# One FFN head weighted by ScalarE in two passes, its sums partly made by VectorE, and the expert Gelu in one burst

## The chip, the cores and the metric

The kernel runs on one core of a Trainium2 chip. The time is that of one execution on the device, in microseconds (us); of the kernel before there are three runs, with a median of 1721.02 us (1718.32 to 1722.32). The engines of the core work in parallel, each through its own list of instructions, and meet at semaphores: TensorE (PE), VectorE (DVE), ScalarE (ACT), GpSimd (POOL) and SyncE (SP, which issues the transfers).

## What is computed

A transformer block over 16 sequences of 512 tokens with 128 channels, in fp32: windowed attention, then an FFN that picks experts by product keys. Only the FFN is touched by the change:

```python
xn = (x - mu) * rsqrt(var + eps) * gamma + beta          # over all rows
q = (xn @ w_q.T)...                                      # 2 halves, 8 heads
sim = einsum('pbnhd,hkpd->pbnhk', q, keys)               # 32 similarities per half and head
s, i = top_k(sim, 8)
all_scores = sx[..., :, None] + sy[..., None, :]         # pair sums of the two halves
scores, pk = top_k(all_scores, 8)                        # 8 of the 1024 experts per head
o = einsum('bnd,bnhkd->bnhk', inputs, key_in[idx])
o = gelu(o) * softmax(scores)
return einsum('bnhk,bnhkd->bnd', o, key_out[idx])
```

The kernel gathers nothing. For each token and head it makes all 1024 pair sums, gives each the weight exp(sum - max - ln Z) where the sum is at least the eighth largest and zero elsewhere, adds the weights of the 8 heads, multiplies them with Gelu of all 1024 expert products, and multiplies the result with key_out.

## The kernel before

The attention runs first (to about 700 us) and isn't touched. The FFN, function `ffn`, works on 64 tiles of 128 tokens, in 16 groups (`GROUPS`) of four tiles (`GT`); k is the tile's place in its group and j its number. Each engine runs the same loops, over groups, k and the heads h = 0 to 7, and what an engine does besides its main work is written by hand into slots: "at head h of tile k, first do this".

- POOL (L772 in `pair_sums`) makes the 1024 pair sums of each head from the tile's similarities SIM into one of 16 buffers SUM. It may write a buffer when the mask of the head 16 before is done (`sum_buffer_free`, L776).
- ScalarE (L873) makes exp(sum + bias) into one of two PSUM buffers E, with the bias NB of that head. It waits for the sum, and for the mask two heads before, which frees E. In its slots: the copy of the similarities (`sim_copy`, L800), the copy of the output (`finish`, L820), two copies of expert products per tile (`o_copy`, L811), twice per group a Gelu over four expert blocks with a table load before and after it (`gelus`, L806, L807), the small exp (L837) and the logarithm (L841) of the next tile's softmax, and once per group the normalised rows BNT (L815).
- VectorE (L965, called the mask here) compares the sums with the eighth largest (TOP) and multiplies by E, into one of eight buffers W. Its other work is `choose`, cut into parts, for the tile ahead: parts 0 to 3 are the sixteen sweeps of max-8 over 32 similarities (L909), part 4 the candidates (L916 to L921), part 5 the eight largest and their distance from the maximum, D8 (L926, L929), part 6 the sum Z (L932), part 7 the bias NB (L936). `EVEN_PARTS` and `ODD_PARTS` say at which head which part is done: an entry (1, 0) is part 0 for the next tile. `experts` (L948), at head 1, multiplies the weights of the tile before, which TensorE has turned and added in WT, with the Gelu values GE, into CT. M8X and TOP lie in PSUM (SMALL).
- TensorE turns each W into WT, eight transposes a head (L1033), and in its slots makes the similarities (L975), one expert block of 512 tokens at a time (`o_block`, L978) and the output product (L997, L1000). Similarities, expert blocks and output all pass through one PSUM bank, MB. WT has one buffer: the first transposes of a tile wait until CT of the tile before has been made.
- SP loads the rows and the turned rows of the next group and stores the outputs of the last (L754, L759, L763).

The expert products of the first group are made before the loops, in the E buffers, and read by Gelu straight from PSUM (L828, L988).

Of the kernel before, what the change touches and what calls it, by code (L numbers as in the profile page):

```python
# [29 lines left out]
ACT = mybir.ActivationFunctionType  # L30
# [634 lines left out]
WRING = 8  # L665

EVEN_PARTS = ((), (), (), (), ((1, 0), (1, 1), (1, 2), (1, 3), (1, 4), (1, 5), (2, 0), (2, 1)), (), ((1, 6),), ((1, 7),))
ODD_PARTS = ((), (), ((1, 2),), ((1, 3),), ((1, 4), (1, 5)), (), ((1, 6),), ((1, 7),))

SIM0 = 2  # L670
SLOT_A, SLOT_OUT, SLOT_SIM, SLOT_B = 0, 2, 4, 6
COPY_B, COPY_A, COPY_OUT, COPY_SIM = 1, 3, 5, 7


def ffn(nc, ctx, x1, x2T, KM, key_in, key_out, gb, ident, bnst, first, out):
# [6 lines left out]
    def sem(name):  # L682
# [23 lines left out]
    NB = [sb(f"NB{b}", [P, FH]) for b in range(2)]  # L706
    SUM = [sb(f"SUM{b}", [P, NE]) for b in range(RING)]
# [6 lines left out]
    SMALL = ps("SMALL", [P, 4, FH, TOPK])  # L714
# [5 lines left out]
             "experts_weighted out_product out_copied expert_product expert_copied gelu_ready "  # L720
             "out_stored ranked candidates top_ready top_less_max top_exp exp_sum log_sum bias_ready").split()
# [46 lines left out]

    def pair_sums(eng, j, h, q):
# [26 lines left out]
    def _(act):  # L796
# [5 lines left out]
        def gelus(g, b, half):  # L802

            act.wait_ge(S["expert_copied"], g * BLK + (half + 1) * 4)
            o = GE[b][:, 4 * half:4 * half + 4, :].rearrange("p e n -> p (e n)")
            nc.scalar.activation(o, o, ACT.Gelu).then_inc(S["gelu_ready"], 1)  # L806
            nc.scalar.preload_act_table_set("natural_log_exp_and_others")  # L807

        def o_copy(g, b, e):
            act.wait_ge(S["expert_product"], g * BLK + e + 1)  # L810
            nc.scalar.copy(GE[b][:, e, :], MB[:, :]).then_inc(S["expert_copied"], 1)  # L811
# [17 lines left out]
        act.wait_ge(S["expert_copied"], BLK)  # L829
        act.sem_inc(S["gelu_ready"], 2)  # L830
# [8 lines left out]
        def small_ln(j):  # L839
            act.wait_ge(S["exp_sum"], j + 1)  # L840
            nc.scalar.activation(LZ[:, :], Z[:, :], ACT.Ln).then_inc(S["log_sum"], 1)  # L841

# [3 lines left out]
        def group(g, b, more):  # L846
            for k in range(GT):
# [4 lines left out]
                for h in range(FH):  # L852
# [6 lines left out]
                    if h == COPY_B and k and more:  # L859
                        o_copy(g + 1, 1 - b, 2 * k - 1)  # L860
# [237 lines left out]
```

## Time and profile before

| | us |
|---|---|
| median of three runs | 1721.02 |
| profiled execution, its time | 1717.66 |
| its span, first to last instruction | 1715.9 |
| busy in the span: VectorE | 1502.3 |
| TensorE matmul | 1490.5 |
| POOL | 1330.6 |
| ScalarE | 1264.6 |
| costliest groups: pair sums on POOL (L772), 512 of them | 958.5 |
| masks on VectorE (L965), 512 | 641.9 |
| exps on ScalarE (L873), 512 | 566.6 |

The profile is of one execution. Busy time is the union of an engine's instructions, so instructions that overlap are counted once. A timeline row gives the start of an instruction (or of a run of like ones, xN), the time to the end of the last, and in brackets the time that the engine stood idle before it and what ended that. Releasers are inferred from semaphore events. The step from one instruction's start to the next one's is often shorter than the duration, because engines start the next while the last drains; where an engine is full, the steps add up to its time and the durations don't. The granted clock is TensorE's, in parts of 2.4 GHz.

### The profile page before, as it was taken

Reading aid. Unit: us, or ns where it says so; the run is one execution under the profiler, and the core shown is the slowest. Engines: PE = TensorE matmul, PEld = TensorE weight load, DVE = VectorE, ACT = ScalarE, POOL = GpSimd, SP = SyncE. Lnnn points to the kernel's source line nnn. Section 1 sums busy time; section 2 is a strip of 40 time slices with the busy share of each in tenths; the row PEclk is TensorE's granted clock in tenths of the full one; section 3 lists DMA queues with packets and bytes.
Section 4 is the critical chain, followed back from the end, with each engine's and each line's share of the span. In section 5 each row is a group of like instructions: output and inputs, shape, how many; then the busy total and the mean of one; then the engine's idle time right before and its main releaser. Section 6 shows DMA issues by size and latency. Waiting matters only on the chain.

```text
span 1715.9 us, 33034 instructions
## 1 busy us (share of the span) xinstructions
PE 1490.5 (87%) x10688; PEld 1029.4 (60%) x10688; DVE 1502.3 (88%) x4488; ACT 1264.6 (74%) x1741; POOL 1330.6 (78%) x1579
## 2 busy tenths in 40 slices
PE   3799999999999998678888888888888888888877
PEld 2355555555555554367667666676666766667766
DVE  3889999999999985389999999999999999999998
ACT  1166666666666666378888888888888888888885
POOL 1055555556655556499999999999999999999993
PEclk9799999999999999789999999999999999999999
DMA  5344445444555440100000000000000000000000
GB/s 139 88 99 105 109 111 118 111 110 103 119 113 111 103 103 22 62 1 19 1 20 20 1 19 19 7 13 19 19 1 20 20 1 19 19 8 13 14 7 7
DMA packets 73627, 86.37 MB, mean 50 GB/s; under 512 B 9872, under 2 KB 63760, under 8 KB 68752
## 3 DMA queue, kind: packets, MB, share of 16 engines
q1 hardware_dynamic: 73456, 84.27, 20.7%
q8 instruction: 85, 1.39, 0.4%
q14 instruction: 86, 0.70, 0.2%
HBM read 58.30 MB, written 25.95 MB: 49 GB/s over the span
## 4 chain that ended last, share of the span: by engine, by line
POOL 47%; issue 5%; ACT 3%; DVE 2%; PE 1%; ACTq 0%; DVEq 0%; SPq 0%
POOL SUM L772 47%; ACT E L873 2%; DVE W L965 2%; ACT L807 1%; ACT GE L806 0%; PE WT L1033 0%; PE MB L1000 0%; PE E L988 0%; DVE CT L948 0%; DVE M8Y L909 0%; DVE SMALL L926 0%; ACT L806 0%; ACT SIM L800 0%; PE MB L975 0%; DVE SMALL L909 0%
## 5 line engine op out<-in xcount | busy, mean ns | idle before, releaser
L772 POOL TENSOR_TENSOR SUM<-SIM 128x1024 f32<-128x1024 f32 x512 | 958.5, 1928 | 11.5 <-DVE W L965 7.9
L965 DVE SCALAR_TENSOR_TENSOR W<-SUM,SMALL,E 128x1024 f32<-128x1024 f32 x512 | 641.9, 1279 | 46.4 <-ACT E L873 44.7
L873 ACT ACTIVATE E<-SUM,NB 128x1024 f32<-128x1024 f32 x512 | 566.6, 1118 | 102.1 <-DVE W L965 86.9
L1033 PEld LDWEIGHTS WT<-idf,W 128*128 128x128 f32 x4096 | 497.3, 151 | 231.3 <-DVE W L965 120.6
L1033 PE MATMUL WT<-idf,W 128*128 128x128 f32 x4096 | 570.8, 292 | 69.3 <-DVE CT L948 38.0
L261 POOL TENSOR_SCALAR_AFFINE_SELECT PT<-PT 128x128 f32<-128x128 f32 (+1 forms) x1024 | 336.9, 355 | 257.8 <-ACT PT L355 224.2
L414 DVE CUSTOM_DVE_ANT_0 SY<-SY,bandf 128x384 f32<-128x384 f32 x512 | 273.3, 574 | 0.0
L355 ACT ACTIVATE PT<-TX 128x512 f32<-128x512 f32 x256 | 153.0, 598 | 113.6 <-PE TX L542 113.4
L429 DVE TENSOR_REDUCE mx<-SX 128x2 f32<-128x512 f32 x256 | 174.5, 682 | 59.8 <-PE SX L524 59.7
L357 ACT ACTIVATE PT<-TY 128x768 f32<-128x768 f32 x256 | 207.4, 810 | 3.7
L570 PE MATMUL PV<-PT,V 128*32 128x384 f32 (+1 forms) x2048 | 165.5, 441 | 2.6 <-POOL PT L261 2.4
L516 PE MATMUL SY<-K,Q 72*128 72x384 bf16 x512 | 144.0, 339 | 8.4 <-DVE mx L414 4.3
L542 PE MATMUL TY<-Q,K 75*128 75x384 bf16 x512 | 125.9, 328 | 11.5 <-ACT PT L357 10.4
L975 PE MATMUL MB<-KM,BNT 128*128 128x512 f32 x128 | 72.1, 645 | 71.2 <-ACT OUT L820 69.4
L1000 PE MATMUL MB<-KO,CT 128*128 128x128 f32 x1024 | 124.9, 275 | 1.1 <-DVE CT L948 1.1
L516 PE MATMUL SX<-K,Q 72*128 72x256 bf16 x512 | 102.0, 281 | 24.4 <-DMA Q<-q_parts 18.9
L1000 PEld LDWEIGHTS MB<-KO,CT 128*128 128x128 f32 x1024 | 119.5, 192 | 1.3 <-DVE CT L948 1.3
L542 PE MATMUL TX<-Q,K 75*128 75x256 bf16 x512 | 99.6, 276 | 3.9 <-ACT PT L355 2.7
L948 DVE TENSOR_TENSOR CT<-WT,GE 128x1024 f32<-128x1024 f32 x64 | 78.4, 1225 | 20.2 <-PE WT L1033 20.2
L542 PEld LDWEIGHTS TX<-Q,K 75*128 75x128 bf16 x512 | 37.6, 98 | 97.2 <-issue 82.2
L570 PEld LDWEIGHTS PV<-PT,V 128*32 128x32 f32 x2048 | 53.6, 109 | 68.1 <-issue 47.9
L516 PEld LDWEIGHTS SX<-K,Q 72*128 72x128 bf16 x512 | 48.7, 100 | 67.3 <-issue 18.6
(110 smaller groups left out, 1638.9 us busy)
## 6 DMA issues: line engine op xcount, KB each, us to landing
K<-k_parts SPq DMA_DIRECT2D x96, 192.0 KB
Q<-q_parts SPq DMA_DIRECT2D x288, 64.0 KB
q_parts<-qp SPq DMA_DIRECT2D x16, 384.0 KB, 2.4
k_parts<-kp SPq DMA_DIRECT2D x16, 384.0 KB, 2.4
xin<-in_x SPq DMA_DIRECT2D x16, 256.0 KB, 3.1
xres<-in_x SPq DMA_DIRECT2D x16, 256.0 KB, 9.5
x<-X SPq DMA_DIRECT2D x16, 256.0 KB, 2.2
x2T<-X2T SPq DMA_DIRECT2D x16, 256.0 KB, 2.1
```

Of the source, the lines that this page charges most:

```text
L261: return nc.gpsimd.affine_select(out=out, in_=out, compare_op=ALU.is_ge, fill=0.0, base=0, pattern=([[0, 2]] if pairs else []) + [[s, P]], ...
L357: nc.scalar.activation(pt[:, 512:1280].rearrange("p (j n) -> p j n", j=2), TY[:, :, 0:384], ACT.Exp).then_inc(S["inner_exp"], 1)
L414: return nc.vector.tensor_tensor_reduce(out=scores, in0=scores, in1=bandf[:, k0 * P:k1 * P], scale=1.0, scalar=-3e38, op0=ALU.add, op1=ALU ...
L429: nc.vector.tensor_reduce(mx[:, h, 0:4:3], SX[:, :, :], AX.X, ALU.max).then_inc(S["outer_maxima"], 1)
L516: return pe.matmul(out, Q[b][0:KQ, h, i * P:(i + 1) * P], K[b][0:KQ, h, k0 * P:k1 * P], start=clear, stop=done, skip_group_check=True)
L542: return pe.matmul(out[:, 0:(q1 - q0) * P], K[b][0:R, h, j * P:(j + 1) * P], Q[b][0:R, h, q0 * P:q1 * P], start=True, stop=True, skip_grou ...
L570: o = pe.matmul(PV[32 * e:32 * e + 32, q0 * P:q1 * P], V[b][:, slot:slot + SLOT_V], PT[:, h % 8, at:at + (q1 - q0) * P], start=(j == 0 and ...
L772: return eng.tensor_tensor(SUM[(q * FH + h) % RING][:, :].rearrange("p (i j) -> p i j", i=NK), sx, sy, ALU.add)
L873: nc.scalar.activation(E[h % 2][:, :], SUM[(k * FH + h) % RING][:, :], ACT.Exp, bias=NB[q][:, h:h + 1]).then_inc(S["exp_ready"], 1)
L965: nc.vector.scalar_tensor_tensor(out=W[h % WRING][:, :], in0=SUM[(k * FH + h) % RING][:, :], scalar=TOP[q][:, h, TOPK - 1:TOPK], in1=E[h % ...
L1000: o = pe.matmul(po, CT[k % 2][:, e, :], key_out[:, e, :], start=False, stop=(e == BLK - 1))
L1033: o = pe.matmul(WT[:, e, :], W[h % WRING][:, e * P:(e + 1) * P], ident[:, :], is_transpose=True, start=(h == 0 and e % 4 == 0), stop=(h == ...
```

## The change

One head of the eight, LH = 3, is no longer masked by VectorE. ScalarE reads its sums in place with Prelu, bias minus the eighth largest (NT) and alpha 1e30, so that sums below the eighth largest become hugely negative and the others their distance from it; then exp with the bias NL, which is D8 of the eighth largest less ln Z, writes W directly. VectorE makes the two biases: NT in part 5, NL in part 7. There are so seven masks a tile, and the exps of a tile alternate over the two E buffers by their own count.

In the tiles with k = 3 and k = 0 (tile 0 excepted, 31 in all) the pair sums of that head are made by VectorE and not by POOL, in two new parts: part 8 copies the 32 similarities of one half to PSUM (XL), part 9 makes the 1024 sums from XL and SIM.

The expert products of the next group are no longer made two a tile through MB and copied. At k = 2, after head 0's exp, TensorE makes all eight one after another in the halves of the two E buffers (`experts_in`), and ScalarE, between two table loads, reads each with Gelu into GE (`experts_gelu`). To go with it, the ranking parts are placed anew: three tables instead of two, with a long list at head 1 of tile k = 2. SP's list isn't changed.

```diff
+LH = 3
+MASKED = FH - 1
+SUMS_AHEAD = (2, 3)
+BURST = 2
+NORMAL_PARTS = ((), (), ((1, 0), (1, 1)), ((1, 2), (1, 3)), ((1, 4), (1, 5)), (), ((1, 6),), ((1, 7),))
+BURST_PARTS = ((), ((1, 0), (1, 1), (1, 2), (1, 3), (1, 4), (1, 5), (1, 8), (2, 0), (2, 1), (2, 2), (2, 3), (2, 4), (1, 9)), (), (), (), (), ((1, 6),), ((1, 7),))
+LATER_PARTS = ((), (), ((1, 8),), ((1, 9),), ((1, 5),), (), ((1, 6),), ((1, 7),))
+PARTS = (NORMAL_PARTS, NORMAL_PARTS, BURST_PARTS, LATER_PARTS)
...
+    XL = SMALL[:, 4, 0:NK // TOPK, :].rearrange("p a b -> p (a b)")
...
     def sum_buffer_free(eng, j, h):
-        wait_pos(eng, S["weights_masked"], j * FH + h - RING + 1)
+        if h == LH:
+            wait_pos(eng, S["l_weights"], j - 1)
+        else:
+            wait_pos(eng, S["weights_masked"], masked(j - 2, h))
...
                 for h in range(FH):
+                    if h == LH and sum_by_vector(j):
+                        continue
                     sum_buffer_free(pool, j, h)
...
+        def experts_gelu(j, g, b):
+
+            wait_pos(act, S["experts_weighted"], (g - 1) * GT)
+            nc.scalar.preload_act_table_set("gelu_and_others")
+            for e in range(BLK):
+                act.wait_ge(S["expert_product"], g * BLK + e + 1)
+                nc.scalar.activation(GE[b][:, e, :], expert_bank(j, e), ACT.Gelu).then_inc(S["expert_copied"], 1)
             nc.scalar.preload_act_table_set("natural_log_exp_and_others")
+            act.wait_ge(S["expert_copied"], (g + 1) * BLK)
...
+        def l_shift(j, k, q):
...
+            s = SUM[(k * FH + LH) % RING][:, :]
+            nc.scalar.activation(s, s, ACT.Prelu, bias=NT[q][:, :], alpha=1e30).then_inc(S["l_shifted"], 1)
+
+        def l_exp(j, k, q):
+
+            act.wait_ge(S["l_shifted"], j + 1)
+            wait_pos(act, S["weights_turned"], (j - 1) * FH + LH + 1)
+            nc.scalar.activation(W[LH][:, :], SUM[(k * FH + LH) % RING][:, :], ACT.Exp, bias=NL[q][:, :]).then_inc(S["l_weights"], 1)
...
+                    if h == 1 and k == BURST and more:
+                        experts_gelu(j, g + 1, 1 - b)
...
+                    if h == LH - 1:
+                        l_shift(j, k, q)
+                    if h == LH:
+                        l_exp(j, k, q)
...
+                nc.vector.tensor_scalar(NT[q][:, :], TOP[q][:, LH, TOPK - 1:TOPK], -1.0, None, ALU.mult)
...
             if part == 7:
                 dve.wait_ge(S["log_sum"], j + 1)
-
+                nc.vector.tensor_tensor(NL[q][:, :], D8[:, LH, TOPK - 1:TOPK], LZ[:, LH:LH + 1], ALU.subtract)
...
+            if part == 8 and sum_by_vector(j):
+
+                nc.vector.tensor_copy(XL, SIM[r][:, 0, LH, :]).then_inc(S["l_x_moved"], 1)
+            if part == 9 and sum_by_vector(j):
+
+                dve.wait_ge(S["l_x_moved"], sums_by_vector(j))
+                wait_pos(dve, S["l_weights"], j - 1)
+                nc.vector.tensor_tensor(SUM[(r * FH + LH) % RING][:, :].rearrange("p (i j) -> p i j", i=NK),
+                                        XL.unsqueeze(2).broadcast_to([P, NK, NK]),
+                                        SIM[r][:, 1, LH, :].unsqueeze(1).broadcast_to([P, NK, NK]), ALU.add).then_inc(S["l_sums"], 1)
...
+        def experts_in(j, g, b):
+
+            for e in range(BLK):
+                if e == 0:
+                    pe.wait_ge(S["x2T_loaded"], (g + 1) * 16)
+                    pe.wait_ge(S["weights_masked"], j * MASKED)
+                if e == 2:
+                    pe.wait_ge(S["weights_masked"], j * MASKED + 1)
+                if e >= 4:
+                    pe.wait_ge(S["expert_copied"], g * BLK + e - 3)
+                pe.matmul(expert_bank(j, e), key_in[:, e * P:(e + 1) * P], X2T[b][:, :], start=True, stop=True).then_inc(S["expert_product"], 1)
```

## Rows read from the trace of the kernel before

**Rows 1.** The page: busy time of each engine, and the chain that ended last.

```profile
PE 1490.5 (87%) x10688; PEld 1029.4 (60%) x10688; DVE 1502.3 (88%) x4488; ACT 1264.6 (74%) x1741; POOL 1330.6 (78%) x1579
...
POOL 47%; issue 5%; ACT 3%; DVE 2%; PE 1%; ACTq 0%; DVEq 0%; SPq 0%
```

**Rows 2.** Timeline of POOL; columns: start us, length us, engine, line, operation, count, idle.

```profile
720.35 636.25 POOL L772 TENSOR_TENSOR SUM<-SIM 128x1024 f32<-128x1024 f32 x340 [3.54 <-ACT SIM L800]
...
1357.30 29.98 POOL L772 TENSOR_TENSOR SUM<-SIM 128x1024 f32<-128x1024 f32 x16 [0.70 <-DVE W L965]
```

**Rows 3.** Timeline of DVE, two tiles of the steady state (same columns).

```profile
1344.14 2.48 DVE L965 SCALAR_TENSOR_TENSOR W<-SUM,SMALL,E 128x1024 f32<-128x1024 f32 x2 [0.49 <-ACT E L873]
...
1346.61 1.23 DVE L948 TENSOR_TENSOR CT<-WT,GE 128x1024 f32<-128x1024 f32 x1
...
1347.75 3.81 DVE L965 SCALAR_TENSOR_TENSOR W<-SUM,SMALL,E 128x1024 f32<-128x1024 f32 x3
...
1351.48 0.84 DVE L909 MAX8 SMALL<-SIM 128x8 f32<-128x32 f32 x8
...
1354.69 0.84 DVE L909 MAX8 SMALL<-SIM 128x8 f32<-128x32 f32 x8
...
1355.94 2.49 DVE L965 SCALAR_TENSOR_TENSOR W<-SUM,SMALL,E 128x1024 f32<-128x1024 f32 x2 [0.41 <-ACT E L873]
...
1358.47 1.28 DVE L965 SCALAR_TENSOR_TENSOR W<-SUM,SMALL,E 128x1024 f32<-128x1024 f32 x1
...
1360.33 2.48 DVE L965 SCALAR_TENSOR_TENSOR W<-SUM,SMALL,E 128x1024 f32<-128x1024 f32 x2 [0.50 <-ACT E L873]
```

**Rows 4.** Timeline of ACT over the same two tiles.

```profile
1350.26 1.28 ACT L806 ACT_TABLE_LOAD   x1
...
1351.56 1.91 ACT L806 ACTIVATE GE<-GE 128x2048 f32<-128x2048 f32 x1
...
1354.78 1.12 ACT L873 ACTIVATE E<-SUM,NB 128x1024 f32<-128x1024 f32 x1
...
1359.18 2.16 ACT L873 ACTIVATE E<-SUM,NB 128x1024 f32<-128x1024 f32 x2
...
1361.65 0.59 ACT L811 COPY GE<-MB 128x512 f32<-128x512 f32 x1 [0.32 <-PE MB L978]
```

**Rows 5.** Timeline of ACT at the start of the FFN.

```profile
721.41 0.60 ACT L828 ACTIVATE GE<-E 128x512 f32<-128x512 f32 x1 [0.26 <-PE E L988]
...
724.84 0.60 ACT L828 ACTIVATE GE<-E 128x512 f32<-128x512 f32 x1 [0.26 <-PE E L988]
```

**Rows 6.** Timeline of PE over the two tiles of Rows 3.

```profile
1350.24 1.95 PE L1000 MATMUL MB<-KO,CT 128*128 128x128 f32 x16
...
1356.24 1.39 PE L975 MATMUL MB<-KM,BNT 128*128 128x512 f32 x2 [2.30 <-ACT OUT L820]
...
1357.43 3.33 PE L1033 MATMUL WT<-idf,W 128*128 128x128 f32 x16
...
1361.45 1.91 PE L1033 MATMUL WT<-idf,W 128*128 128x128 f32 x16
```

**Rows 7.** Windows, PE: length us, busy us (instructions), granted clock, DMA share, GB/s.

```profile
1357.50:1358.00 0.50, 0.50 (x4) 0.50 1.01 281
```

**Rows 8.** Instructions of two lines of the attention: duration ns min/median/max.

```profile
L404 DVE SCALAR_TENSOR_TENSOR rm<-MB,mp x32: 274/274/278, 63.7 to 664.7; 32x128 f32<-32x128 f32 x32
...
L410 DVE TENSOR_TENSOR mp<-rm,mp x32: 274/354/510, 67.1 to 667.0; 32x128 bf16<-32x128 f32 x32
```

**Rows 9.** Timeline of DVE and POOL in the attention.

```profile
365.39 0.69 DVE L477 TENSOR_TENSOR qp<-rq,qp 128x512 bf16<-128x512 f32 x1
...
366.07 0.55 POOL L261 TENSOR_SCALAR_AFFINE_SELECT PT<-PT 128x128 f32<-128x128 f32 x2 [0.78 <-ACT PT L355]
```

**Rows 10.** Timeline of DVE, last group of four tiles.

```profile
1651.18 2.48 DVE L965 SCALAR_TENSOR_TENSOR W<-SUM,SMALL,E 128x1024 f32<-128x1024 f32 x2 [0.49 <-ACT E L873]
...
1709.62 1.23 DVE L948 TENSOR_TENSOR CT<-WT,GE 128x1024 f32<-128x1024 f32 x1 [1.19 <-PE WT L1033]
```

More of the change, by code:

```diff
@@ L706, in ffn @@
     NB = [sb(f"NB{b}", [P, FH]) for b in range(2)]
+    NT = [sb(f"NT{b}", [P, 1]) for b in range(2)]
+    NL = [sb(f"NL{b}", [P, 1]) for b in range(2)]
     SUM = [sb(f"SUM{b}", [P, NE]) for b in range(RING)]
@@ L767, in _, with sum_by_vector, sums_by_vector, sums_by_pool @@
         store(GROUPS - 1, 1)
+    def sum_by_vector(j):
+        return j > 0 and (j - 1) % GT in SUMS_AHEAD
+    def sums_by_vector(j):
+        return sum(sum_by_vector(i) for i in range(j + 1))
+    def sums_by_pool(j, h):
+        return j * FH + h + 1 - sums_by_vector(j if h >= LH else j - 1)
+    def masked(j, h):
+        return j * MASKED + (h if h >= LH else h + 1)
+    def expert_bank(j, e):
+        return E[(j * MASKED + 1 + e // 2) % 2][:, e % 2 * GN:(e % 2 + 1) * GN]
     def pair_sums(eng, j, h, q):
@@ L857, in group @@
                         bnt(g + 1, 1 - b)
-                    if h == COPY_B and k and more:
-                        o_copy(g + 1, 1 - b, 2 * k - 1)
-                    if h == COPY_B and not k and real:
-                        o_copy(g, b, BLK - 1)
-                    if h == COPY_A and more:
-                        if k == 0:
-                            wait_pos(act, S["experts_weighted"], g * GT)
-                        o_copy(g + 1, 1 - b, 2 * k)
+                    if h == 1 and k == BURST and more:
+                        experts_gelu(j, g + 1, 1 - b)
                     if h == COPY_OUT and (real or k):
@@ L878, in group @@
                         small_ln(j + 1)
-                    if (k, h) == (2, 3) and more:
-                        gelus(g + 1, 1 - b, 0)
-                    if (k, h) == (0, 3) and real:
-                        gelus(g, b, 1)
         steps(act, group)
@@ L945, in experts @@
             dve.wait_ge(S["weights_turned"], (j + 1) * FH)
-            dve.wait_ge(S["gelu_ready"], (g + 1) * 2)
+            dve.wait_ge(S["expert_copied"], (g + 1) * BLK)
             wait_pos(dve, S["out_product"], j - 1)
@@ L956, in group @@
                 for h in range(FH):
-                    for ahead, part in (ODD_PARTS if k % 2 else EVEN_PARTS)[h]:
+                    if h == 1 and real:
+                        experts(*prev)
+                    for ahead, part in PARTS[k][h]:
                         if more or k < GT - ahead:
                             choose(part, j + ahead, (k + ahead) % 4, (k + ahead) % 2)
-                    if h == 1 and real:
-                        experts(*prev)
-                    dve.wait_ge(S["exp_ready"], j * FH + h + 1)
+                    if h == LH:
+                        continue
+                    n = masked(j, h)
+                    dve.wait_ge(S["exp_ready"], n)
                     wait_pos(dve, S["weights_turned"], j * FH + h - WRING + 1)
                     nc.vector.scalar_tensor_tensor(out=W[h % WRING][:, :], in0=SUM[(k * FH + h) % RING][:, :], scalar=TOP[q][:, h, TOPK - 1:TOPK],
-                                                   in1=E[h % 2][:, :], op0=ALU.is_ge, op1=ALU.mult).then_inc(S["weights_masked"], 1)
+                                                   in1=E[(n - 1) % 2][:, :], op0=ALU.is_ge, op1=ALU.mult).then_inc(S["weights_masked"], 1)
         steps(dve, group)
```

53 lines of the change are left out of this document (21 added, 32 removed).

## The prediction, made before the changed kernel was run

> **What bounds the kernel now.** I read the page first. Its chain of work that ended last gives POOL 47% of the span [rows 1], so at first sight the pair sums of POOL are the bound and every sum taken off it is time won. The timeline of POOL says otherwise. The first 340 sums of the FFN run without a gap in 636.25 us, 1.87 us each, which is 15.0 us for the eight of a tile; after that POOL runs 16 sums in 29.98 us and then stands 0.70 us until the mask of L965 frees a buffer of the ring of 16, and this pair of tiles, 30.68 us, repeats to the end [rows 2]. So POOL was ahead from the start, filled its ring, and is then held back by its consumer: the FFN runs at 15.34 us a tile, set by VectorE and ScalarE together, not at POOL's 15.0.
>
> The timeline of VectorE shows how these two hold each other. The exps go into two PSUM buffers, so an exp may start only when the mask two before it has ended. One mask takes 1.28 us, and the next instruction starts 1.20 us after it; an exp takes 1.12 us and the next starts 1.04 us after it [rows 3, 4]. With masks alone this loop keeps up (1.2 to 1.27 us a head). Whatever ScalarE does between two exps, while VectorE has nothing but masks, is lost: 1.86 us instead of 1.2 pass from mask 6 (1358.47) to mask 7 (1360.33; mask h is that of head h, 0 to 7), because a logarithm and a copy of 512 columns stand between the exps [rows 3]. Where VectorE has other work, ScalarE's extra is hidden: two table loads and a Gelu of 2048 columns, from 1350.26 to 1354.78, cost VectorE only 0.41 us [rows 3, 4].
>
> **The change, part by part.** I lay out one group of four tiles, counting each tile from the start of one mask 7 to the start of the next; four tiles take 61.4 us now (twice 30.68). Steps come from rows 3 unless another group is named. After mask 7: 1.20 to the next tile's mask 0, 1.27 to the expert product CT (L948), 1.14 to mask 1. The ranking for the next tile (parts 0 to 5) takes 3.21 (1351.48 to 1354.69), about 0.8 of it for each eight max-8 (0.84) and 1.6 for candidates and top. Mask 4 to mask 6: 2.53 (1355.94 to 1358.47).
>
> *Head 3 moved to ScalarE.* Per tile it takes one mask, 1.20, off VectorE and adds there two instructions of one column, which I take at 0.1 each, the step of one max-8 (what the second may wait for is costed below). ScalarE gets two passes of 1.04 in place of one. In an ordinary tile these are hidden: VectorE then has CT, 1.14, and 3.2 us of ranking between its masks.
>
> *Ordinary tiles (k = 0 and 1).* 1.20 + 1.27 + 1.14 + 1.20 (mask 1) + 0.80 + 1.20 (mask 2) + 0.85 + 0.65 + 1.00 (ranking, with the new small instruction) + 2.53 (mask 4 to mask 6) + 1.86 = 13.7 us each. ScalarE is ready in time: exp 1 begins at 1.35, when mask 7 has ended, the shift pass at 2.4, exp 2 runs from 3.45 to 4.6, and mask 2 comes at 5.6.
>
> *Sums made by VectorE (for k = 3 and k = 0, 31 in all).* Each takes 1.87 off POOL, which is worth nothing by itself, since POOL is not the bound. It costs VectorE a tensor_tensor of 1024 columns with one input in PSUM, like CT (1.23, step 1.14), and a copy of 32 columns, about 0.12. Tile k = 3: 1.20 + 1.27 + 1.14 + 1.20 + 0.12 + 1.20 + 1.14 (sum) + 0.95 (part 5) + 2.53 + 1.86 = 12.6.
>
> *The Gelu burst (k = 2).* Eight copies of 0.59, two Gelus of 1.91 and four table loads per group go; eight Gelus of 0.60 and two loads come. That is 6 us less ScalarE work a group, but now it stands in one piece in which no exp can be made, because its products lie in the exps' own PSUM buffers. TensorE: the transposes of head 7 begin when mask 7 has ended, at 1.35, and take 0.95 (16 in 1.91 [rows 6]); then eight products. At the start of the FFN the same products come to ScalarE's Gelu one each 0.857 us (721.41 to 724.84 is four) [rows 5], not one each 0.5 as ScalarE could take them. The last Gelu so ends at 2.3 + 7 x 0.857 + 1.02 + 0.64 = 10.0, the load after it at 11.3 (1.28 to 1.31 for a load) [rows 4], exp 1 at 12.45 (1.02 is one product alone: 0.86 and the last pass's tail, and 0.64 the Gelu with its start). VectorE has meanwhile done mask 0, CT and the ranking moved here (3.3 + 2.0 + 0.2 + the sum of 1.14), and is idle from 10.2 to 12.45. After that ScalarE is behind and VectorE has masks alone: shift pass, exp 2, second pass, exp 4 follow at 1.05 each, so that mask 4 comes at 16.7; the copy of OUT waits for transposes (0.95) and output products (2.2) that TensorE starts only when mask 1 has ended at 13.8, so it comes at 17.0, mask 5 at 18.3, mask 6 at 19.6, and after logarithm and copy of SIM mask 7 at 21.4 [rows 4, 6]. So 21.4 us.
>
> Sum of a group: 13.7 + 13.7 + 12.6 + 21.4 = 61.4 us, against 61.4 now. What three tiles win, the burst tile loses. At the ends: group 0 wins 0.2 (its first tile has no CT), the last group has no burst: 13.7 + 13.2 (no copy of SIM) + 14.5 (the ranking for k = 3 and its sum, 4.6 us, ahead of mask 1, then masks paced by the exps) + 11.9 (no ranking) = 53.3, against 56.0 now (1651.18 to the last CT at 1709.62, less the 2.47 between mask 7 and CT [rows 10]), so 2.7. By these steps alone: 3 us less.
>
> *TensorE's clock.* After the burst TensorE stands idle from 10.25 to 13.8, 3.5 us. In the kernel before, after a standstill of 2.30 us, the granted clock is 0.50 (1.2 instead of 2.4 GHz) and 16 transposes take 3.33 us instead of 1.91 [rows 6, 7]. There this lies beside work that hides it. In the burst tile it lies on the path: the OUT copy, the fifth exp and all behind it wait. Price between 0 and 1.8 us; I take the row's difference, 1.4, in 15 groups: +21 us.
>
> *The new bias NL (part 7 of choose).* This one-column tensor_tensor reads D8 and LZ, both in SBUF. No VectorE instruction of the FFN does so now while POOL is at work: each has one input in PSUM. The attention shows what it means. L404 and L410 have one shape, 32x128; L404 (one input in PSUM) takes 274 to 278 ns, L410 (both in SBUF) 274 to 510, median 354; it is the longer where a POOL instruction of 0.4 us is under way [rows 8]. And where L477, both in SBUF, runs for 0.69 us from 365.39, POOL's next instruction begins at 366.07, at its end [rows 9]. So they exclude each other for a whole instruction. The Trainium skill, "SBUF — State Buffer", section "Who interferes with whom", says the same: a VectorE instruction with two SBUF inputs and a GpSimd one that reads SBUF share a read interface, and whichever starts first keeps it to its end. In the FFN a POOL instruction lasts 1.87 us and the next follows at once. NL waits between 0 and 1.87; mask 7 (now 1.86 after mask 6, of which 1.2 is mask 6 itself) and, through NB, the next tile's exp absorb 0.4 of it. Over an even spread the mean of what is left is 1.47 squared / 2 / 1.87 = 0.58 us a tile, 37 us in 64 tiles. Bounds: 0 (POOL idle at that point, or one column too short to matter) and 1.47 x 64 = 94.
>
> Forecast: 1717.7 (the profiled execution) - 3 + 21 + 37 = 1773. The median of the runs lies 3.4 above that execution, so 1776.
>
> One rule speaks against the burst more strongly still. A load here is followed by its activation within 0.03 us (1350.26 + 1.28, next 1351.56) [rows 4]. The Trainium skill, "ScalarE: Activation LUTs", section "What ACT_TABLE_LOAD costs", adds 1.38 us of drain to each; with that the two loads of a burst would cost 2.8 us more on the path, some 41 us in all. The row decides; I leave it out.
>
> **Rivals.**
> (a) Only the clock, no lock: an instruction of one column slips in between. 1717.7 + 18, as a median 1739. For it: nothing so short is in the trace beside a busy POOL. Chance 0.20.
> (b) Neither: TensorE's pause falls so that the clock stays up. 1718 as a median, within 0.2%. Chance 0.08.
> (c) Faster: ScalarE isn't late after the burst. If the masks after it came at VectorE's pace, the burst tile would cost its VectorE work, 7 x 1.20 + 1.14 + 6.6 + 0.5 = 16.6, plus the 2.3 of standstill, 18.9 instead of 21.4: 15 x 2.5 = 37 us less, about 1680 without the lock. Against it: the 1.05 of each exp and two extra passes are plain rows. Chance 0.13.
> (d) The lock at its worst: POOL's and VectorE's periods lock in a bad phase, a wait near 1.87 in most tiles: 1773 + 40 = 1813 and up. Chance 0.07.
> (e) Prelu isn't in the set that holds exp and logarithm: two loads a tile, 64 x 2.6 = 166 us more, about 1900. No row shows a Prelu. Chance 0.04.
> Forecast itself 0.48.
>
> **How the numbers follow.** A difference of 0.2% is about what a measurement of this kernel can tell from none. Slower: forecast 0.48, (a) 0.20, (d) 0.07, (e) 0.04, less a little that falls near zero, 0.76. Same: most of (b), 0.07. Faster: (c) and the rest of (b), 0.17. Range 1714 to 1812: from (b) to the edge of (d); it leaves out (c), (e) and part of (d), about 2 in 10.
>
> **What would show it.** Right: groups of 63 to 66 us in VectorE's timeline; in tile k = 2 masks 1, 2 and 4 at 12.5, 14.6 and 16.7 after the mask 7 before; transposes after the burst at a granted clock of 0.5; NL with durations spread from 0.16 to 2 us; POOL idle some 5 us or more a group. Wrong: NL at 0.16 everywhere (then a); products in the burst faster than 0.857; a table load at the Prelu's line; POOL without idle time, which would mean that its sums bound the kernel after all.

## The result and the profile of the kernel after

The changed kernel takes 1866.84 us (median of four runs, 1865.28 to 1866.94). The kernel before, run beside it on the same chip, takes 1719.67 (1713.83 to 1722.32). The ratio is 1.0859, with a 95% interval of 1.0829 to 1.0888: 147 us slower. The forecast was 1776 in a range of 1714 to 1812: right in direction and in the two causes it named, too low by 91 us.

The page of the kernel after: busy time, granted clock in 40 slices, the chain that ended last, and the groups that matter.

```profile
PE 1507.1 (81%) x10688; PEld 1072.1 (57%) x10688; DVE 1595.7 (86%) x4614; ACT 1235.8 (66%) x1745; POOL 1274.8 (68%) x1548
...
PEclk9799999999999997789889889889889889889888
...
PE 22%; DVE 21%; issue 15%; ACT 4%; DVEq 0%; ACTq 0%; SPq 0%
...
L802 POOL TENSOR_TENSOR SUM<-SIM 128x1024 f32<-128x1024 f32 x481 | 904.5, 1914 | 209.9 <-DVE W L1023 206.1
L1095 PE MATMUL WT<-idf,W 128*128 128x128 f32 x4096 | 566.7, 293 | 273.6 <-DVE W L1023 203.0
...
L979 DVE TENSOR_TENSOR NL<-D,LZ 128x1 f32<-128x1 f32 x64 | 135.9, 2123 | 0.3 <-ACT LZ L873 0.3
```

Beside [rows 1] three things stand out. VectorE is busy for 1595.7 us in place of 1502.3, although it lost 64 masks: 135.9 us of that are 64 instructions on one column each (L979, the new bias NL), which therefore last 2.12 us on average. The chain no longer runs through POOL at all. And POOL stands idle for 206 us in its sums' line, held back by the masks (L1023).

The timeline of VectorE shows what NL does. Columns as in the rows of before: start, length, engine, line, operation, count, idle before it.

```profile
1300.80 1.18 DVE L979 TENSOR_TENSOR NL<-D,LZ 128x1 f32<-128x1 f32 x1
...
1313.77 1.29 DVE L1023 SCALAR_TENSOR_TENSOR W<-SUM,SMALL,E 128x1024 f32<-128x1024 f32 x1
1314.97 5.70 DVE L979 TENSOR_TENSOR NL<-D,LZ 128x1 f32<-128x1 f32 x1
1320.59 0.15 DVE L980 SCALAR_TENSOR_TENSOR NB<-LZ,SMALL 128x8 f32<-128x8 f32 x1
1320.66 2.54 DVE L1023 SCALAR_TENSOR_TENSOR W<-SUM,SMALL,E 128x1024 f32<-128x1024 f32 x2
1323.99 1.23 DVE L1003 TENSOR_TENSOR CT<-WT,GE 128x1024 f32<-128x1024 f32 x1 [0.79 <-PE WT L1095]
...
1335.93 0.77 DVE L979 TENSOR_TENSOR NL<-D,LZ 128x1 f32<-128x1 f32 x1
```

POOL over the same stretch.

```profile
1286.95 33.70 POOL L802 TENSOR_TENSOR SUM<-SIM 128x1024 f32<-128x1024 f32 x18 [1.37 <-DVE W L1023]
1322.01 3.78 POOL L802 TENSOR_TENSOR SUM<-SIM 128x1024 f32<-128x1024 f32 x2 [1.36 <-DVE W L1023]
```

The NL that starts at 1314.97 ends at 1320.67, and POOL's run of 18 sums ends at 1320.65: VectorE has stood still while POOL ended one sum and made three more. The NL at 1300.80 ends at 1301.98, eight sums of 1.87 after 1286.95: it waited for the running sum alone. NL never ends anywhere but at the end of a sum, unless POOL stands idle (once, 0.15 us). Of the 64, 51 take between 0.77 and 1.78 us, eleven 5.69 to 5.72, and one, at 755.71 when POOL still fills its ring, 18.75. Everything behind it waits too: the exps stand idle for NB, 104.7 us in all.

The burst tile (k = 2): ScalarE, then TensorE, then VectorE.

```profile
1337.95 1.28 ACT L840 ACT_TABLE_LOAD   x1
1340.02 0.60 ACT L843 ACTIVATE GE<-E 128x512 f32<-128x512 f32 x1 [0.79 <-PE E L1045]
...
1346.03 0.60 ACT L843 ACTIVATE GE<-E 128x512 f32<-128x512 f32 x1 [0.26 <-PE E L1045]
1346.64 1.28 ACT L844 ACT_TABLE_LOAD   x1
1347.94 1.12 ACT L920 ACTIVATE E<-SUM,NB 128x1024 f32<-128x1024 f32 x1
```

```profile
1350.43 1.09 PE L1095 MATMUL WT<-idf,W 128*128 128x128 f32 x8 [3.57 <-DVE W L1023]
...
1351.62 3.54 PE L1067 MATMUL MB<-KO,CT 128*128 128x128 f32 x16
```

```profile
1349.09 1.28 DVE L1023 SCALAR_TENSOR_TENSOR W<-SUM,SMALL,E 128x1024 f32<-128x1024 f32 x1 [2.17 <-ACT E L920]
1351.16 1.29 DVE L1023 SCALAR_TENSOR_TENSOR W<-SUM,SMALL,E 128x1024 f32<-128x1024 f32 x1 [0.79 <-ACT E L920]
1353.24 1.28 DVE L1023 SCALAR_TENSOR_TENSOR W<-SUM,SMALL,E 128x1024 f32<-128x1024 f32 x1 [0.79 <-ACT E L920]
1356.52 1.28 DVE L1023 SCALAR_TENSOR_TENSOR W<-SUM,SMALL,E 128x1024 f32<-128x1024 f32 x1 [2.00 <-ACT E L920]
```

Here the layout of the prediction is found step by step: a Gelu each 0.859 us, paced by its product, as in [rows 5]; VectorE idle for 2.17 us, forecast 2.3; then masks 2.07 apart, forecast 2.1; TensorE idle for 3.57 us, forecast 3.5, and behind that pause a granted clock of 0.50 (a window from 1352.0 to 1354.5), at which the output product takes 3.54 us in place of 1.95. The eight transposes right behind the pause still ran at 0.98 (a window from 1350.0 to 1351.6); the low clock came after them. A load is followed by its exp after 1.30 us, as in [rows 4]; the 1.38 us of drain that the Trainium skill adds in "ScalarE: Activation LUTs", section "What ACT_TABLE_LOAD costs", are in no load of the burst either. The Prelu starts at 1348.99, 1.05 us after that exp, with no load at its line, so rival (e) is out, and the masks 2.07 apart rule out rival (c).

### The profile page after: what moved, and what is told of

Its sections match the earlier page's. It is cut to its first block, busy times and chain, and to the rows that moved or that the text cites. A ratio compares the mean times of both kernels' runs of the same rounds, so it can differ in the third digit from the quotient of the medians.

```text
span 1865.2 us, 32977 instructions
## 1 busy us (share of the span) xinstructions
PE 1507.1 (81%) x10688; PEld 1072.1 (57%) x10688; DVE 1595.7 (86%) x4614; ACT 1235.8 (66%) x1745; POOL 1274.8 (68%) x1548
## 4 chain that ended last, share of the span: by engine, by line
PE 22%; DVE 21%; issue 15%; ACT 4%; DVEq 0%; ACTq 0%; SPq 0%
DVE W L1023 12%; PE WT L1095 10%; PE E L1045 6%; PE MB L1067 5%; ACT E L920 3%; DVE NL L979 2%; DVE CT L1003 1%; DVE SMALL L969 1%; DVE SMALL L952 1%; DVE M8Y L952 1%; PE MB L1064 1%; DVE SUM L989 1%; DVE Z L976 1%; DVE NB L980 1%; PE E L1055 0%
## 5 line engine op out<-in xcount | busy, mean ns | idle before, releaser
L802 POOL TENSOR_TENSOR SUM<-SIM 128x1024 f32<-128x1024 f32 x481 | 904.5, 1914 | 209.9 <-DVE W L1023 206.1
L1023 DVE SCALAR_TENSOR_TENSOR W<-SUM,SMALL,E 128x1024 f32<-128x1024 f32 x448 | 569.5, 1279 | 114.8 <-ACT E L920 114.5
L920 ACT ACTIVATE E<-SUM,NB 128x1024 f32<-128x1024 f32 x448 | 498.7, 1114 | 134.7 <-DVE NB L980 104.7
L1067 PE MATMUL MB<-KO,CT 128*128 128x128 f32 x1024 | 149.9, 309 | 1.1 <-DVE CT L1003 1.1
L1067 PEld LDWEIGHTS MB<-KO,CT 128*128 128x128 f32 x1024 | 146.5, 228 | 1.3 <-DVE CT L1003 1.3
L979 DVE TENSOR_TENSOR NL<-D,LZ 128x1 f32<-128x1 f32 x64 | 135.9, 2123 | 0.3 <-ACT LZ L873 0.3
L854 ACT COPY OUT<-MB 128x128 f32<-128x128 f32 x64 | 17.0, 265 | 143.2 <-PE MB L1067 143.2
L843 ACT ACTIVATE GE<-E 128x512 f32<-128x512 f32 x120 | 71.7, 597 | 42.1 <-PE E L1045 42.1
```

The lines of the kernel that those rows point to most:

```text
L802: return eng.tensor_tensor(SUM[(q * FH + h) % RING][:, :].rearrange("p (i j) -> p i j", i=NK), sx, sy, ALU.add)
L920: nc.scalar.activation(E[(n - 1) % 2][:, :], SUM[(k * FH + h) % RING][:, :], ACT.Exp, bias=NB[q][:, h:h + 1]).then_inc(S["exp_ready"], 1)
L1023: nc.vector.scalar_tensor_tensor(out=W[h % WRING][:, :], in0=SUM[(k * FH + h) % RING][:, :], scalar=TOP[q][:, h, TOPK - 1:TOPK], in1=E[(n ...
L1067: o = pe.matmul(po, CT[k % 2][:, e, :], key_out[:, e, :], start=False, stop=(e == BLK - 1))
```

## The experiments

Three suspects: NL's wait for POOL, TensorE's clock, and the rest of the reordering. A tile's time below is the distance of its CT (L1003) from the CT before, read from VectorE's timeline; four are a group, given in the order k = 2, 3, 0, 1.

### e1: NL without a second SBUF input

The first one-column operand of NL is put into PSUM, by one more instruction of one column in part 5.

```diff
+    DP = SMALL[:, 4, NK // TOPK, 0:1]
...
+                nc.vector.tensor_tensor(DP, TOP[q][:, LH, TOPK - 1:TOPK], CD[:, LH, 0:1], ALU.subtract)
...
-                nc.vector.tensor_tensor(NL[q][:, :], D8[:, LH, TOPK - 1:TOPK], LZ[:, LH:LH + 1], ALU.subtract)
+                nc.vector.tensor_tensor(NL[q][:, :], DP, LZ[:, LH:LH + 1], ALU.subtract)
```

> The changed kernel with one thing different: the bias NL is made from the distance of the eighth largest in PSUM (one more one-column instruction in part 5) and ln Z in SBUF, so that it has one SBUF input. Theory 1 (the whole loss beyond the forecast is the wait of this instruction for POOL): its mean falls from 2.12 us to about 0.15 us, the waits of 5.7 and 18.8 us vanish, and the time falls by some 105 to 125 us of 1867, to 1740 to 1760, where my sum without the lock had 1739. Rival (the long durations only cover other waits, for exps or ring buffers, which then show up elsewhere): the time falls by less than 40 us.

Measured 1768.5 us, ratio to before 1.0296 (1.0277 to 1.0316). Every NL now takes 0.15 us; the row gives duration min/median/max:

```profile
L981 DVE TENSOR_TENSOR NL<-SMALL,LZ x64: 150/152/157, 729.4 to 1743.2; 128x1 f32<-128x1 f32 x64
```

That is 97 us less, by (1.0859 - 1.0296) x 1719, where 105 to 125 were expected. So the lock costs 97 us in this kernel, whatever it does to TensorE's clock included. The same from the durations: 135.9 less 64 x 0.15 is 126 us of waiting, of which 97 reach the end, so that 29 us, 0.45 a tile, are absorbed (the prediction had 0.4). But 1768 is 50 us above before, where a clock term of 21 and a gain of 3 had left room for 18. Its steady tiles take 22.97, 14.0, 14.0 and 13.9, 64.9 a group.

### e2: the lock alone, in the kernel before

The kernel before with that one instruction added in part 7; nothing reads its result.

```diff
+                nc.vector.tensor_tensor(NL[q][:, :], D8[:, 3, TOPK - 1:TOPK], LZ[:, 3:4], ALU.subtract)
```

> The kernel before with one instruction added, the same one-column tensor_tensor of two SBUF inputs in part 7 of each tile (its result is used by nothing). Theory 1, first half (it waits for the end of the POOL instruction under way, 1.87 us at most): mean duration about 1.0 us, 0.6 us a tile lost, 1720 to about 1757. Theory 1, second half (if it comes just before such an end it misses it, and then gets no turn until POOL itself pauses): some durations of many times 1.87 us, more so early, where POOL has the ring to fill; mean 2 us or more, time 1790 or more. Rival (the cost belongs to something else of the change): durations of 0.16 us and about 1723.

Measured 1773.49 us, ratio 1.0328 (1.0302 to 1.0354). The 64 add up to 115 us: nearly all are 1.42 to 1.44 and 1.70 to 1.73 by turns, and one is 18.52. The steady tiles go from 13.90 and 16.82 to 14.96 and 16.95, so they lose 1.06 and 0.13, 0.6 on average. The prediction's formula gives 0.58 for a wait of at most one sum, but from an even spread of waits with 0.4 absorbed, and neither is found here: that the two agree is luck. 0.6 a tile is 37 us; the one long wait accounts for the other 19.

```profile
759.66 18.52 DVE L936 TENSOR_TENSOR NL<-D,LZ 128x1 f32<-128x1 f32 x1
```

```profile
738.90 39.26 POOL L773 TENSOR_TENSOR SUM<-SIM 128x1024 f32<-128x1024 f32 x21
779.52 3.78 POOL L773 TENSOR_TENSOR SUM<-SIM 128x1024 f32<-128x1024 f32 x2 [1.36 <-DVE W L966]
```

759.66 + 18.52 is 778.18, the end of POOL's run is 778.16. The ring held sums that POOL could go on making without VectorE, and it made them all. This NL began 1.71 us before the next end of a sum, so a start just before an end is not what brings a long wait on.

### e3: are VectorE's sums worth anything?

e1 with all sums on POOL again (no head in which VectorE makes them).

```diff
-SUMS_AHEAD = (2, 3)
+SUMS_AHEAD = ()
```

> As e1, but no sums by VectorE: POOL makes all 512. Theory: with the lock gone, a group takes about 61 to 63 us, POOL needs 60.0 for its 32 sums, so POOL is nearly the bound; VectorE saves two sums and two copies, 2.5 us a group, of which about 1.2 (tile k = 3, where it is full) would have been on the path, and POOL's limit takes it back: within 10 us of e1. Rival (POOL's sums bound the kernel, as its chain of before suggests): 30 us or more slower than e1.

Measured 1769.6 us, ratio 1.0313 (1.0292 to 1.0334): the same as e1. (The profiled run is the fastest of the five, 1756.9; the others took 1767 to 1772.) POOL makes 512 sums instead of 481 and still stands idle for its consumer, so it never was the bound, as the prediction had read from [rows 2]. This run shows something else as well. It runs two of its early groups in 61.4 us each (21.39, 12.59, 13.71, 13.72) and all from 1186 us on in 64.9 (22.97, 13.99, 14.00, 13.90), with the same instructions in the same order. What differs is the clock: 1.00 over the first two, 0.89 over the later ones.

### e4: TensorE kept busy in the pause after the burst

e1 with four products of 512 columns on TensorE, added work without use, written to the free bank MB after the expert products and head 0's transposes in the burst tile.

```diff
+FILL = 4
...
+                    if h == 1 and k == BURST and more:
...
+                        for _ in range(FILL):
+                            pe.matmul(MB[:, :], ident[:, :], key_in[:, 0:GN], start=True, stop=True)
```

> As e1, with four products of 512 columns added on TensorE into the idle bank MB, in the burst tile between head 0's and head 1's transposes, 3.4 us of work in a pause of 3.6 us; their result is overwritten. Theory (the low clock after the pause costs 1.4 us a group): output product after the burst in 1.95 us, not 3.54; 15 to 25 us faster than e1. Rival (the late exps after the burst are set by ScalarE's own work, not by the output product): same as e1 within 4 us.

Measured 1724.34 us, ratio 1.0045 (1.003 to 1.006), mean granted clock 0.979 (e1 0.933). Its tiles are 21.39, 12.66, 13.71 and 13.72: the prediction's 21.4, 12.6, 13.7 and 13.7. So the layout had every tile right, and the low clock costs (1.0296 - 1.0045) x 1718 = 43 us in e1, not 21. Where, the timeline of TensorE shows, first e1, then e4.

```profile
1325.78 3.49 PE L1097 MATMUL WT<-idf,W 128*128 128x128 f32 x16 [1.41 <-DVE CT L1005]
...
1349.57 1.97 PE L1097 MATMUL WT<-idf,W 128*128 128x128 f32 x8 [3.57 <-DVE W L1025]
```

```profile
1336.54 2.19 PE L1103 MATMUL WT<-idf,W 128*128 128x128 f32 x16 [1.41 <-DVE CT L1006]
...
1349.25 2.19 PE L1103 MATMUL WT<-idf,W 128*128 128x128 f32 x16 [1.41 <-DVE CT L1006]
```

At the change of tiles TensorE stands for 0.7 us and then for 1.41, waiting for CT. In e1 the 16 transposes behind that ran at 0.50 of the clock (a window from 1326.0 to 1329.0) and took 3.49 us, in e4 2.19 at 1.00 (1336.6 to 1338.7). CT and the output copy sit behind those too. The fill in the burst tile removes the low clock not only there but at nearly all tile changes. In e1 its burst tile loses 22.97 - 21.39 = 1.6 us (the prediction had 1.4) and the three others 14.0 - 12.66, 14.0 - 13.71 and 13.9 - 13.72 = 1.8 us: the half that the prediction did not have.

In the kernel after itself, with the lock in place, the low clock lies in part elsewhere. A tile change like these runs at 1.00 there (a window from 1305.9 to 1308.0), and the 0.50 (1322.1 to 1331.0) stands behind the pause that a long wait of NL makes:

```profile
1305.81 2.19 PE L1095 MATMUL WT<-idf,W 128*128 128x128 f32 x16 [1.41 <-DVE CT L1003]
...
1321.99 1.97 PE L1095 MATMUL WT<-idf,W 128*128 128x128 f32 x8 [5.79 <-DVE W L1023]
1325.37 3.65 PE L1095 MATMUL WT<-idf,W 128*128 128x128 f32 x16 [1.41 <-DVE CT L1003]
```

So 97 and 43 are the two losses taken out in this order. No run of the changed kernel has the lock without the low clock, and in the other order the split could differ.

### e5: NL a little later

The kernel after with two instructions of one column, which touch no second SBUF input, ahead of NL.

```diff
+                for i in range(2):
+                    nc.vector.tensor_scalar(NX[:, 2 * q + i:2 * q + i + 1], TOP[q][:, LH, TOPK - 1:TOPK], -1.0, None, ALU.mult)
```

> The changed kernel, with two one-column instructions of VectorE (PSUM to SBUF, result unused) ahead of NL, which moves NL 0.14 us later. In the changed kernel the waits of 5.7 us all begin 0.07 us before a POOL instruction ends, and all others begin at least 0.6 us before one and end with it. Theory 1 (a request that comes just before the end of a POOL instruction misses it and then gets no turn until POOL pauses): moved past that end, these waits become 1.8 us, NL's sum falls from 136 us to 80 to 105, and the kernel gets 25 to 50 us faster in spite of the added work. Rival (the long waits belong to that tile, k = 1, or to a long stream of POOL, and not to the moment): they stay at 5.7 us and the time is that of the changed kernel or a few us more.

Measured 1870.95 us, ratio 1.0881 (1.0842 to 1.0921). The theory was that the long waits are a matter of 0.1 us, because in the kernel after the long-waiting NLs start 0.08 to 0.10 us ahead of the end of a sum. It fell. They now start 0.07 to 0.11 after the next sum has begun, and wait to the same point as before:

```profile
1323.91 5.56 DVE L982 TENSOR_TENSOR NL<-D,LZ 128x1 f32<-128x1 f32 x1
```

```profile
1295.76 33.70 POOL L803 TENSOR_TENSOR SUM<-SIM 128x1024 f32<-128x1024 f32 x18 [2.45 <-DVE W L1026]
```

(1323.91 + 5.56 = 1329.47, 1295.76 + 33.70 = 1329.46.) Again eleven of 5.55 to 5.58, and one of 18.61.

### e8: POOL with fewer sums ready

The kernel after; each of POOL's sums waits for the masks of two heads more than its buffer needs.

```diff
+LESS = 2
...
-        else:
-            wait_pos(eng, S["weights_masked"], masked(j - 2, h))
+        wait_pos(eng, S["weights_masked"], masked(j - 2, h) + LESS)
```

> The changed kernel; GpSimd alone is held back: before each sum it waits for the weights of two heads more than its data needs, so that fewer sums with their waits already met stand ready on its queue. In the changed kernel 12 of the 64 NL operations got their turn only after three or more of GpSimd's operations (5.7 us eleven times, 18.75 once), and in all of these GpSimd had at least three ready sums; where at most two were ready VectorE got its turn at the end of the running operation. Theory A, the length of the wait is the number of sums that stand ready: the waits of 5.7 us and the long one vanish, NL's sum falls from 136 us to some 60 to 90, and the time from 1867 to some 1810 to 1835 us. Theory B, the length comes from the place in the group (a group's second tile), not from what stands ready: the eleven waits of 5.7 us stay, NL's sum stays over 120 us and the time within 15 us of 1867. GpSimd's smaller lead can cost some us of its own, since each of its sums starts later by two heads; the sums' readers (the next layer's projections) show it if it does.

Measured 1872.38 us, ratio 1.0907 (1.0876 to 1.0939). (The sums' readers are ScalarE's exps; there is no next layer here.) Neither theory holds as put. The waits of 5.7 us are gone, as A said, but their sum isn't down: 131.7 us. In their place stand 15 waits of 3.50 to 3.84 us, ten of 1.96 to 1.99 and one of 15.01. What holds is the end of the long ones: all 16 over 3 us end within 0.03 us of the end of an unbroken run of POOL, behind which it stands idle for its next mask. That it takes three ready sums is wrong, since here one or two went ahead of VectorE; and in the kernel after the first two NLs waited for one end only (1.78 and 1.24 us) with about ten sums ready. The ten waits of 1.96 to 1.99 are a third kind: NL starts some 0.08 us before the end of a sum, is passed over there, and gets its turn at the next end, although POOL has more sums ready.

```profile
894.78 1.96 DVE L979 TENSOR_TENSOR NL<-D,LZ 128x1 f32<-128x1 f32 x1
```

```profile
877.99 35.55 POOL L803 TENSOR_TENSOR SUM<-SIM 128x1024 f32<-128x1024 f32 x19 [0.21 <-DVE W L1023]
```

The tenth sum of this run ends at 896.7, the NL at 896.74, and nine more sums follow without a gap. One more thing differs in this kernel: the sum of head 3 has two waits ahead of it, the others one. Wherever that sum came next at the end of the one under way, NL got its turn (30 times, these ten among them); the long waits end elsewhere, behind sums with one wait.

### e9: shorter instructions on POOL

The kernel after with each sum made by two instructions of 512 columns.

```diff
...
+        n = NK // 2
+        for a in (0, n):
+            sx = SIM[q][:, 0, h, a:a + n].unsqueeze(2).broadcast_to([P, n, NK])
...
+            last = eng.tensor_tensor(SUM[(q * FH + h) % RING][:, a * NK:(a + n) * NK].rearrange("p (i j) -> p i j", i=n), sx, sy, ALU.add)
```

> The changed kernel with each of GpSimd's pair sums made by two instructions of 512 columns each, of which only the second reports; same data, same waits, same places. It shows whether NL's wait is counted in GpSimd's instructions or in the work that stands ready. Theory A, a number of instructions passed over: every wait halves, the eleven of 5.70 us become some 2.9, the sum of the 64 falls from 136 us to some 70, and the time by some 45 to 55 us, to 1815. Theory B, VectorE, once passed over, gets its turn only when GpSimd has nothing ready: the waits of 5.7 us stay (three sums ready are six instructions), only the short ones (54 us in all, 0.77 to 1.8 each, the rest of one instruction) halve; the sum is about 108 us and the time about 1845. Against either: if one half takes over 0.95 us the sums cost GpSimd more than 1.87 us each, and over some 1.8 in place of 1.87 for two halves its slack of a group shrinks; at 1.05 a half GpSimd (30 sums a group, 63 us) is still under a group's 72 us.

Measured 1901.71 us, ratio 1.1077 (1.1022 to 1.1131): slower yet, against both. POOL makes a half each 1.01 us. The 64 NL add up to 156.3 us. The short waits did halve: 48 of them are 0.15 to 0.94. There are more long ones: fifteen of 4.77 to 8.60, and 24.26 at the start.

```profile
1338.66 8.58 DVE L982 TENSOR_TENSOR NL<-D,LZ 128x1 f32<-128x1 f32 x1
```

```profile
1311.01 36.21 POOL L804 TENSOR_TENSOR SUM<-SIM 128x512 f32<-128x512 f32 x36 [1.22 <-DVE W L1026]
1348.59 4.06 POOL L804 TENSOR_TENSOR SUM<-SIM 128x512 f32<-128x512 f32 x4 [1.37 <-DVE W L1026]
```

1338.66 + 8.58 = 1347.24, POOL's run ends at 1347.22, and nine of its instructions have ended in between. So the long wait is not a number of instructions: all 16 end with POOL's run, as in theory B (e8's ten short passings stay the exception). B's time (1845) is missed: more NLs are passed over (16 instead of 12), and two halves take 2.01 us in place of 1.87, so that POOL's run of ready work is longer. How much each of the two adds was not separated. Two NLs of this run had the same picture before them, 0.75 us to the next end and four halves ready, and waited 4.78 us (at 897.13) and 0.76.

### e6b, e6, e7: the rest of the loss, and a version that beats both

All three have e1's NL. e6b also makes the burst tile's output product right after head 0's transposes and no longer behind those of head 1, so that it is itself the work that fills TensorE's pause. e6 besides moves the two passes of head 3 ahead of the Gelus. e7 besides puts one product of 512 columns without use ahead of head 0's transposes in the other tiles.

```diff
                     if h == 1 and k == BURST and more:
+                        l_shift(j, k, q)
+                        l_exp(j, k, q)
                         experts_gelu(j, g + 1, 1 - b)
...
-                    if h == SLOT_OUT and real:
+                    if h == (1 if k == BURST and more else SLOT_OUT) and real:
...
+                        if real and not (k == BURST and more):
...
+                            for _ in range(FILL):
+                                pe.matmul(MB[:, :], ident[:, :], key_in[:, 0:GN], start=True, stop=True)
```

> As e1 (NL with one input in PSUM), and in the burst tile TensorE makes the output product one slot earlier, between head 0's and head 1's transposes, in its pause of 3.6 us. Theory: the pause shrinks to about 1.3 us, so the clock stays up behind it, and the OUT copy no longer waits; burst tile 21.1 us instead of 22.97. If the other tiles keep the full clock too, some 1720; if they fall to it as in e1 (14.0 instead of 12.6 and 13.7), up to 1745. Rival (the output product was late for another reason than its place): as e1.

Measured 1719.21 us, ratio 1.001 (0.9993 to 1.0026); burst tile 20.95, against 21.1 expected, and the tile behind it 12.65.

> As e6b_out_early, and in the burst tile both passes of head 3 on ScalarE stand ahead of the Gelu burst instead of behind it. Theory (the burst is paced by TensorE's products, 0.857 us each, so 2.1 us of ScalarE work ahead of it are hidden, and behind it ScalarE is what everything waits for): second exp at 12.45 as now, burst tile 19.3 us, 15 x 1.8 to 2.1 = 27 to 32 us faster than e6b_out_early, about 1690 to 1715 and so faster than the kernel before. Rival (the burst ends later by what is put ahead of it): same as e6b within 5 us.

Measured 1701.95 us, ratio 0.9897 (0.9877 to 0.9918); burst tile 19.45, since two passes that stood among the late exps after the burst are now done in front of it. That is 17 us less than e6b, where 27 to 32 were expected: the burst tile gains 1.5 us and not 1.8 to 2.1, and in four groups the tile k = 3 took 13.99 in place of 12.65.

> As e6_early, and in every other tile TensorE makes one product of 512 columns into the idle bank MB in the pause before head 0's transposes (0.86 us of a pause of 1.41 us; its result is overwritten). Theory (the pauses of 0.66 and 1.41 us around the change of tile are enough to lower the clock when they fall together as they did in e1): mean granted clock up to 0.98 and up to 20 us faster than e6_early, all tiles at 13.7, 12.7 and 19.3. If e6_early has the full clock already: equal to it.

Measured 1693.15 us (1690.26 to 1698.35), ratio 0.985 (0.9824 to 0.9877), clock 0.984; tiles 19.44, 12.65, 13.71 and 13.72, 59.5 a group against 61.4 in before. In e6 some tiles still took 13.99 in place of 12.65; in e7 none of the steady ones does. TensorE's pause of 1.41 us at the tile change is so filled but for 0.1 us on either side of the product:

```profile
1338.95 1.09 PE L1106 MATMUL WT<-idf,W 128*128 128x128 f32 x8 [0.76 <-DVE W L1029]
1340.15 1.13 PE L1102 MATMUL MB<-KI,idf 128*128 128x512 f32 x2
1341.37 2.29 PE L1106 MATMUL WT<-idf,W 128*128 128x128 f32 x16
```

All three ideas of the change are still in e7 (the head on ScalarE, the sums on VectorE, the burst), and with three losses taken out (the lock, the low clock, the late passes after the burst) it is 1.5% faster than the kernel before and 9.3% faster than the kernel after.

## Why the prediction was wrong in size

The 147 us, by the ratios and in the order in which they were taken out: 97 for the lock (e1), 43 for the clock (e4), 8 for the rest. The prediction had 37, 21 and -3.

*The bound.* Right. POOL isn't it: e3 gives its 31 sums back at no cost, and in the kernel after it stands idle for 206 us.

*The layout of the four tiles.* Right, to 0.1 us in each (e4), and with it the sentence that three tiles win what the burst tile loses. The one tile that it had wrong is k = 2 of the last group, which has no burst: 14.5 forecast, 18.93 measured in e1 and e4. There ScalarE stands for the output product, and this behind transposes that TensorE makes at a low clock after a pause of 4.7 us (e4):

```profile
1691.48 1.97 PE L1103 MATMUL WT<-idf,W 128*128 128x128 f32 x8 [4.73 <-DVE W L1026]
...
1693.67 3.05 PE L1070 MATMUL MB<-KO,CT 128*128 128x128 f32 x16
```

The steps for that tile treated the masks as paced by the exps and left out the copy of OUT among them, which the same working had put into the burst tile. These 4.4 us once, a tile of 13.99 in place of 12.66 ahead of the last group, one of 13.91 in the first group, and 0.1 to 0.4 us in some other tiles bring -3 to about +5; the rest, some 3 us, is about the uncertainty of the two medians.

*The clock.* The mechanism was right, the term mis-sized: 21 forecast, 43 measured. The pause after the burst was placed and priced correctly (1.4 forecast, 1.6 measured). But the change also removed the two expert blocks of each tile from TensorE, and with them work between head 7 and the next tile. In the kernel before, such a block stands there, between pauses of 0.34 and 0.55 us:

```profile
1345.48 1.09 PE L1033 MATMUL WT<-idf,W 128*128 128x128 f32 x8 [0.34 <-DVE W L965]
1346.41 1.02 PE L978 MATMUL MB<-X2T,KI 128*128 128x512 f32 x2
1347.98 2.19 PE L1033 MATMUL WT<-idf,W 128*128 128x128 f32 x16 [0.55 <-DVE CT L948]
```

Without it the pauses are 0.7 and 1.41 us, and in e1 they were followed by a low clock too. The prediction looked for long pauses only. Its price of 0 to 1.8 for a group counted the burst tile alone.

*The lock.* The mechanism was right, and [rows 8, 9] were the rows to see it in; the failing step is "NL waits between 0 and 1.87", the duration of one POOL instruction. For 52 of the 64 that is what happened. By durations, with the 29 us that e1 leaves as absorbed spread evenly (a way of sharing out the 97, and no second measurement of it): 52 waits sum to 54.4 us; less 0.15 each for the work and 0.45 absorbed, 23 us, 0.45 a tile against a forecast of 0.58. The other twelve last 5.7 us (eleven) and 18.75, and sum to 81.4; less 0.6 each, 74 us. Together 97. In the attention, where [rows 8] come from, L410's wait was never over 0.24 us (510 less 274 ns), beside short instructions of POOL in ones and twos like that of [rows 9]. The FFN's POOL has a queue of ready sums, and all twelve long waits end where such a run ends. Rival (d), the lock at its worst phase, thought of waits near 1.87 in most tiles and had no wait longer than an instruction either; the bound of 94 us for the term happens to lie near the measured 97, for another reason.

The Trainium skill, "SBUF — State Buffer", section "Who interferes with whom", was cited for the exclusion, and every run here agrees: the wait is there with two SBUF inputs (e2, after) and gone with one (e1), for a single column as well. It says that whoever issues first keeps the interface for the whole instruction. Read as the prediction read it, VectorE would by that wait for one instruction at most; the section says nothing of a queue. The runs differ (5.7 and 18.75 us beside sums of 1.87, 8.6 beside halves of 1.01), and they decide.

*What stays open.* Why an NL is passed over at all. Most get the end of the running sum, with at least one further sum ready (51 in after, 62 in e2; in after just one in 38 of them). Of those that are passed over, all with a wait over 3 us wait for POOL to run dry (the twelve of after and of e5, sixteen of e8 and of e9, the one of e2, each within 0.03 us), but ten of e8 got the next end. It isn't the moment of arrival within 0.1 us (e5), nor three or more ready sums (e8), and in e9 moment and ready work were alike for a wait of 4.78 us and one of 0.76. e8's sums with two waits ahead did not pass NL, which points to how early POOL has taken up its next instruction; that was only seen, no run was made for it.

## What to carry to other kernels

A VectorE instruction with both inputs in SBUF, however small, beside a POOL that has a queue of ready work, can cost up to the longest run of ready instructions on POOL, and the upper bound is to be set by that and not by one of them (here 12 of 64 waits were of this kind); one input in PSUM took the price away. Where work is taken off TensorE, list all its pauses before and after, the short ones at stage changes too, since the low clock followed them onto the path here; move existing work into the pause first (the output product in e6b), and only then fill it. And work that is gathered into one burst should have in front of it everything that would otherwise be late behind it (e6).

## What the runs showed of the hardware

- A one-column tensor_tensor with two SBUF inputs took 0.77 to 18.75 us beside POOL, and 0.15 us with one input in PSUM. The whole wait stands in the instruction's duration, and none of it as idle time or as a wait in the profile.
- Every wait over 3 us ended within 0.03 us of the end of an unbroken run of POOL, with up to nine ends of instructions in a steady tile of e9 and 25 in its wait of 24.26 us. Ten waits of 1.96 to 1.99 us in e8 passed one end and got the next. With POOL's work split in two the longest waits of the steady tiles went from 5.7 to 8.6 us, and the kernel was slower by 35 us (1901.71 against 1866.84).
- The granted clock behind a pause of 1.41 us at a tile change was 0.50 in e1 and 1.00 in e4 in the same place of the loop; four products in another tile, 15 us earlier and more, made the difference. In e3 one and the same loop ran its groups in 61.4 us early, at 1.00, and in 64.9 later, at 0.89. So a loop can run at either, and a pause that is filled in one tile can raise the clock in the next ones.
